# A graph-network layer on one core: a new order on ScalarE and VectorE in the edge pass, and a third of the edge dots on VectorE

## The chip, the cores and the metric

The kernel runs on one core of a Trainium2 chip. The metric is the device time of one execution in microseconds (us). TensorE (PE in the profile) multiplies matrices, VectorE (DVE) and ScalarE (ACT) work on rows, GpSimd (POOL) issues the gathers and scatters by index, and SyncE (SP) issues the plain transfers. Every engine works through its own instructions in order and waits on semaphores for the others.

## The reference

50,000 nodes with rows `x` of 256 values, 12,500 edges (`src`, `dst`, a feature row of 128 values each). Two layers, each followed by a normalisation of the rows:

```python
h = x @ Wn.T + bn
e = edge_attr @ We.T + be
a = leaky_relu(sum((h[src] + e) * attn, axis=-1), 0.01)
a = softmax of a over the edges with equal dst
x = layernorm(x + relu(segment_sum(h[src] * a, dst)))
agg = segment_sum(x[dst], src); mean = agg / max(count, 1)
x = layernorm(x + x @ W1.T + b1 + mean @ W2.T + b2)
```

The sum over `e * attn` is the dot of an edge's feature row with the single vector `We.T @ attn`, called u here. The 98 tiles of 128 edges (the last has 84) need one such dot per edge. In the second layer a node that occurs as `src` gets the mean over its neighbours; every other node gets only `x @ W1.T`.

## The kernel before, in words

Edges are handled in T = 100 tiles of 128 (two of them, or nearly so, are padding), four tiles to a group, Q = 25 groups. The program runs through these stages:

1. **Sorting by dst.** VectorE and ScalarE write one-hot tables (`onehots`, `high_onehots`), and TensorE counts them into a histogram (`sort`, `count_tile`). In the same loop TensorE makes the dots of the edge features: `turn_edges` transposes four tiles, ScalarE copies the result out of PSUM (`copy_edges`), `dot_edges` multiplies by u. SyncE loads the feature rows in chunks of eight tiles into the four `yout` buffers (`load_edges`) and puts parts of a copy of x between them (`copy_x`, 125 parts of 400 KB in all). VectorE waits in `edge_dots` for all dots, copies them to `pay`, and then scans the histogram (`starts`). The look-up of each edge's rank follows (`tiles`), and GpSimd scatters the ranked edges.
2. **Sorting by src**, the same without the edge features; GpSimd gathers the rows `x[src]` meanwhile, and VectorE dots them (`v_b`).
3. **DST pass**: softmax, weighted sums by dst, relu, added to the copy of x in DRAM.
4. **Dense pass**: all 98 groups of 512 node rows: normalise, multiply by W1, normalise, store.
5. **SRC pass** (`by_src` on four engines, 25 groups): the mean over neighbours for the nodes that occur as `src`, whose output rows are then overwritten by scatter.

In the SRC pass a step q of TensorE works on two groups. For each half p of a group (two tiles of 128) it transposes the own rows of group h = q - 1 (line 1378, "turn"), sums the neighbours of group q into `bank[2 + p]` (line 1533, "sums"), and multiplies both parts of group h by W2 and W1 (line 1389, "products"). The products of half p wait for ScalarE's copy of the turned rows (`own_copy(p)`, line 586, semaphore `s_tcc`). ScalarE also normalises the own rows (line 770), weighs the neighbour rows (line 750), takes square roots (`root`, line 591) and writes the output rows (`y_rows`, line 596). VectorE takes means and variances (line 971: of own rows, of neighbour rows, of the products), builds the selection matrices (`select_src`, lines 1058 to 1065), computes the scales of the own rows (lines 985 and 801) and adds the carry from tile to tile (`sums_with_carry`, line 801, which waits for the products that read its output before). GpSimd gathers the own rows of a group four steps ahead (line 484) and scatters the finished rows (line 487), eight transfers to a step.

The order on each engine is the order in which the code of `by_src` is written; there is no scheduler. In ScalarE's step the first instruction is the square root for the own rows of group q, which waits for VectorE:

```python
if in_range(q, 0, Q):
    root(u % 2, s_ost, q + 1, s_osq)
own_copy(0)
```

and in VectorE's loop the statistics behind that root come right after `sums_with_carry` of the step before.

## Time and profile before

| | us |
|---|---|
| median of 3 runs (1404.85 to 1406.67) | 1405.91 |
| the profiled execution's own time | 1415.9 |
| its span, first to last instruction | 1414.1 |
| TensorE busy in the span | 1201.5 (85%) |
| VectorE busy | 1002.8 (71%) |
| ScalarE busy | 745.4 (53%) |
| GpSimd busy | 751.7 (53%) |

The profile shows one execution on the chip. Times count from the span's start. The granted clock of TensorE is given as a share of full speed, 1.0 for 2.4 GHz and 0.5 for 1.2 GHz; a stretch that holds some of both shows a value between. The sort by dst takes the span's first 180 us or so, the DST pass runs from about 390 to 600 us, the dense pass from about 615 to 1053 us and the SRC pass from 1056 us to the end.

### The profile page before, as it was taken

What the parts mean: (1) busy time and instruction counts of PE and PEld (TensorE: products, weight loads), DVE (VectorE), ACT (ScalarE), POOL (GpSimd) and SP (SyncE); (2) the same over time, 40 slices, a digit from 0 to 9 for tenths busy, and PEclk for the clock granted to TensorE, in tenths of its full rate; (3) what the DMA queues carried; (4) which work ended last, traced back from release to release, by engine and by line L of the source; (5) the groups of instructions that cost most, each with busy time, mean ns of one, the idle gap of its engine ahead of it and who ended that gap; (6) DMA issues with size and microseconds to landing.
All of it is one profiled execution on the core that took longest, in us unless ns stands there. A gap on an engine that the chain in (4) does not pass through costs nothing.

```text
span 1414.1 us, 25043 instructions
## 1 busy us (share of the span) xinstructions
PE 1201.5 (85%) x6829; PEld 1046.3 (74%) x6829; DVE 1002.8 (71%) x3483; ACT 745.4 (53%) x1743; POOL 751.7 (53%) x731
## 2 busy tenths in 40 slices
PE   5988968991099999949999999999988888888884
PEld 5977857880078888838888888888877777777773
DVE  8377897989455555349999999999985556555551
ACT  3754664550034444427777766667674544545442
POOL 1047772777767777744444106555541555555533
PEclk9989999996589999979999999999998889988887
DMA  6868887979436666657777768999961323222211
GB/s 213 272 150 206 208 225 184 272 231 348 171 68 93 101 94 92 72 137 246 239 240 245 248 241 296 310 321 325 325 238 51 91 94 94 86 91 88 93 47 43
DMA packets 118160, 254.11 MB, mean 180 GB/s; under 512 B 23705, under 2 KB 63272, under 8 KB 118084
## 3 DMA queue, kind: packets, MB, share of 16 engines
q1 hardware_dynamic: 75738, 187.26, 41.8%
q0 software_dynamic: 40128, 64.45, 20.1%
q10 hardware_dynamic: 2218, 1.53, 0.3%
q8 instruction: 30, 0.49, 0.2%
q14 instruction: 46, 0.38, 0.1%
HBM read 175.67 MB, written 130.44 MB: 216 GB/s over the span
## 4 chain that ended last, share of the span: by engine, by line
PE 70%; DVE 11%; DMA 6%; ACT 5%; issue 5%; POOL 1%; SPq 0%; DVEq 0%; ACTq 0%; POOLq 0%
PE bank L1389 41%; PE bank L1378 8%; PE bank L1366 5%; DVE stats L971 4%; PE bank L1438 3%; PE bank L1288 3%; PE bank L1442 3%; DMA X<-in_x,idx_src 3%; DVE X L798 2%; ACT aggn L633 2%; PE bank L1533 2%; ACT sel L687 1%; PE bank L1325 1%; DVE xT L801 1%; DVE xin L798 1%
## 5 line engine op out<-in xcount | busy, mean ns | idle before, releaser
L1389 PE MATMUL bank<-w1T,xT 128*128 128x256 f32 x1968 | 480.3, 392 | 2.0 <-ACT yout L596 2.0
L1389 PEld LDWEIGHTS bank<-w1T,xT 128*128 128x128 f32 x1968 | 378.0, 197 | 56.6 <-ACT xT L586 3.0
L494 POOL DMA_INDIRECT order_scratch<-pay,rank_i x200 | 194.6, 973 | 220.6 <-DVE xin L798 90.3
L586 ACT ACTIVATE xT<-bank 128x512 f32<-128x512 f32 x296 | 176.7, 598 | 91.5 <-PE bank L1378 87.0
L596 ACT ACTIVATE yout<-bank,rstd 128x256 f32<-128x256 f32 x492 | 203.8, 480 | 0.7 <-DVE rstd L1037 0.5
L591 ACT ACTIVATE std<-stats,eps_c 128x4 f32<-128x4 f32 x271 | 80.5, 298 | 230.5 <-DVE stats L971 230.4
L534 POOL DMA_INDIRECT z_scratch<-xin,idx_out x100 | 156.3, 1563 | 53.8 <-ACT xin L713 30.6
L971 DVE BATCH_NORM_STATS2 stats<-bank 128x6 f32<-128x512 f32 x246 | 167.9, 691 | 10.2 <-PE bank L1389 10.1
L971 DVE BATCH_NORM_STATS2 stats<-xin 128x6 f32<-128x512 f32 x240 | 154.6, 686 | 22.6 <-DMA xin<-z_scratch 22.6
L1389 PE MATMUL bank<-w2T,xT 128*128 128x256 f32 x400 | 126.7, 446 | 50.4 <-ACT xT L586 41.8
L487 POOL DMA_INDIRECT out_rows<-yout,idx_out x100 | 102.4, 1024 | 107.7 <-ACT yout L596 83.0
L1366 PE MATMUL bank<-sel,agg 128*128 128x196 f32 x800 | 157.0, 341 | 0.1
L801 DVE SCALAR_TENSOR_TENSOR xT<-csel,xT,bank 128x128 f32<-128x128 f32 x198 | 55.6, 342 | 139.4 <-PE bank L1389 126.3
L1378 PE MATMUL bank<-ident,xin 128*128 128x128 f32 x960 | 128.9, 274 | 19.6 <-DVE xin L798 19.6
L1378 PEld LDWEIGHTS bank<-ident,xin 128*128 128x128 f32 x960 | 114.3, 142 | 34.4 <-issue 19.9
L1389 PEld LDWEIGHTS bank<-w2T,xT 128*128 128x128 f32 x400 | 84.9, 222 | 69.2 <-issue 31.8
L798 DVE TENSOR_SCALAR xin<-xin,stats,rstd 128x256 f32<-128x256 f32 x392 | 136.0, 409 | 0.1
L1366 PEld LDWEIGHTS bank<-sel,agg 128*128 128x128 f32 x800 | 134.4, 196 | 0.6 <-DVE bank L801 0.3
L484 POOL DMA_INDIRECT X<-z_scratch,idx_dst x100 | 96.1, 961 | 69.1 <-DVE xin L798 29.7
L484 POOL DMA_INDIRECT X<-in_x,idx_src x100 | 99.0, 990 | 51.2 <-issue 20.7
L484 POOL DMA_INDIRECT xin<-z_scratch,idx_src x88 | 84.7, 963 | 76.2 <-PE bank L1378 53.8
L1288 PE MATMUL bank<-X 128*128 128x196 bf16 x800 | 96.2, 255 | 28.8 <-ACT sel L687 18.6
(249 smaller groups left out, 1765.7 us busy)
## 6 DMA issues: line engine op xcount, KB each, us to landing
z_scratch<-in_x SPq DMA_DIRECT2D x125, 400.0 KB
xin<-z_scratch SPq DMA_DIRECT2D x97, 512.0 KB, 4.8
out_rows<-yout SPq DMA_DIRECT2D x97, 512.0 KB, 3.7
kB<-sorted_scratch SPq DMA_DIRECT2D x50, 256.0 KB, 3.4
yout<-low_digits_scratch SPq DMA_DIRECT2D x50, 128.0 KB
yout<-keys_scratch SPq DMA_DIRECT2D x50, 128.0 KB, 5.7
yout<-in_edge_attr SPq DMA_DIRECT2D x12, 512.0 KB, 6.2
order_scratch<-pay,rank_i POOLq DMA_INDIRECT x200
```

The costliest lines, as they stand in the source:

```text
L484: g.indirect_dma_start(out=dst_ap, out_offset=None, in_=table, in_offset=where).then_inc(s, 16)
L487: g.indirect_dma_start(out=table, out_offset=where, in_=src_ap, in_offset=None, bounds_check=N - 1, oob_is_err=False).then_inc(s, 16)
L494: g.indirect_dma_start(out=order_dram[k], out_offset=bass.IndirectOffsetOnAxis(ap=rank_i[k][:, t:t + 1], axis=0), in_=pay[:, t, :], in_off ...
L534: g.indirect_dma_start(out=z_dram, out_offset=column(idx_out[DST], GT * q + j), in_=xin[q % 4][:, j, :], in_offset=None, compute_op=ALU.ad ...
L586: a.activation(xT[dst_i][:].rearrange("p a b c -> p (a b c)"), src_bank[:, :], ACT.Copy, bias=raised).then_inc(copied, 1)
L596: a.activation(yout[hu][0:rows, j, :], bank_of(j // 2)[0:rows, (j % 2) * D:(j % 2 + 1) * D], ACT.Copy, scale=rstd[0:rows, slot, j:j + 1]). ...
L798: return v.tensor_scalar(o, i, s1, s2, o0, o1) if o1 is not None else v.tensor_scalar(o, i, s1, s2, o0)
L971: return v.bn_stats(stats[0:rows, slot, 2 * p:2 * p + 2, :].rearrange("p j s -> p (j s)"), pair.rearrange("p j c -> p c j"))
L1288: ins = mm(o[:, b * HC:(b + 1) * HC], onehot_lo[:, t, b * P:(b + 1) * P], onehot_hi[:, t, :], start=False, stop=False, skip_group_check=True)
L1366: ins = mm(bank[3 + t % 4][:, 0:HC], onehotT[n % 2][:, b, j * P:(j + 1) * P], table[i % 2][:, b, :], start=b == 0, stop=b == 1)
L1378: ins = tr(o[:, at:at + n], buf[0:n, 2 * p + jj, c * P:(c + 1) * P], ident[0:n, 0:n])
L1389: ins = mm(to, buf[:, jj, c, 0:n], w[:, c, :], start=not bias and i == 0 and c == 0, stop=i == len(terms) - 1 and c == 1)
```

## The change

It has two parts. In the SRC pass ScalarE and VectorE execute the same instructions in another order. ScalarE's step begins with the copy of the first turned half, and the square root for the own rows is made one group ahead (q + 1 in place of q); the output rows are written in two halves with the second copy between them. VectorE begins its step with the statistics of the products, then takes the own rows' statistics of group q + 1. The first group's own rows are done ahead of the loop.

```diff
+            root(0, s_ost, 1, s_osq)
             weigh_neighbours(0, 0)
...
-                if in_range(q, 0, Q):
-                    root(u % 2, s_ost, q + 1, s_osq)
                 own_copy(0)
-                if in_range(q, 2, Q + 2):
-                    root(2 + u % 2, s_est, q - 1, s_esq)
-                own_copy(1)
                 if in_range(q, 0, Q):
                     act.wait_ge(s_onm, q + 1)
...
+                if in_range(q, 2, Q + 2):
+                    root(2 + u % 2, s_est, q - 1, s_esq)
                 if in_range(q, 0, Q - 1):
-                    weigh_neighbours(q + 1, u + 1)
-                if in_range(q, 0, Q - 2):
-                    root_neighbours(q + 2, u)
+                    root((u + 1) % 2, s_ost, q + 2, s_osq)
                 if in_range(q, 2, Q + 2):
...
-                    y_rows(0, hu, 2 + u % 2, s_ey, lambda p: rbank(u % 2, p))
+                last_step(0)
+                own_copy(1)
+                last_step(1)
+                if in_range(q, 0, Q - 1):
+                    weigh_neighbours(q + 1, u + 1)
+                if in_range(q, 0, Q - 2):
+                    root_neighbours(q + 2, u)
```

One step of ScalarE's queue in the SRC pass, as it was (the step of group 3: `xT2` and `xT3` are the copies of the two turned halves, `std` is a square root, `xin1` the own rows, `X` the weighed neighbours, `yout1` the output rows):

```order
L591 ACTIVATE std<-stats,eps_c 128x4
L586 ACTIVATE xT2<-bank0 128x512
L591 ACTIVATE std<-stats,eps_c 128x4
L586 ACTIVATE xT3<-bank1 128x512
L770 ACTIVATE xin1<-xin1,nmr,rstd 128x256 x4
L750 ACTIVATE X<-X,rstd 128x256 x4
L591 ACTIVATE std<-stats,eps_c 128x4
L596 ACTIVATE yout1<-bank6,rstd 128x256 x2
L596 ACTIVATE yout1<-bank7,rstd 128x256 x2
```

The same step of ScalarE in the changed kernel (lines 600, 785, 605, 610 and 765 are the former 586, 770, 591, 596 and 750):

```order
L600 ACTIVATE xT2<-bank0 128x512
L785 ACTIVATE xin1<-xin1,nmr,rstd 128x256 x4
L605 ACTIVATE std<-stats,eps_c 128x4 x2
L610 ACTIVATE yout1<-bank6,rstd 128x256 x2
L600 ACTIVATE xT3<-bank1 128x512
L610 ACTIVATE yout1<-bank7,rstd 128x256 x2
L765 ACTIVATE X<-X,rstd 128x256 x4
L605 ACTIVATE std<-stats,eps_c 128x4
```

The first copy no longer has a square root ahead of it in its step; the second copy has moved behind the normalising, two square roots and half of the output rows.

VectorE's step of group 2 as it was, up to the first addition of the carry (`aggn` holds own rows, `bank4` and `bank5` products, `X` neighbour rows):

```order
L971 BN_STATS stats<-aggn 128x6 x2
L1058 RECIPROCAL rstd<-std 128x4
L1060 TENSOR_TENSOR rstd<-rstd,weight 128x4
L1063 TENSOR_TENSOR csel1<-kB1,prevk1 128x512
L1065 TENSOR_TENSOR sel1<-kB1,keyc1 128x512
L985 RECIPROCAL rstd<-std 128x4
L801 SCALAR_TENSOR_TENSOR nmr<-stats,rstd 128x4
L971 BN_STATS stats<-bank4 128x6
L971 BN_STATS stats<-bank5 128x6
L971 BN_STATS stats<-X 128x6 x2
L1250 RECIPROCAL rstd<-std 128x4
L801 SCALAR_TENSOR_TENSOR xT0<-csel0,xT1,bank2 128x128 x2
```

and in the changed kernel:

```order
L998 BN_STATS stats<-bank4 128x6
L998 BN_STATS stats<-bank5 128x6
L998 BN_STATS stats<-xin1 128x6 x2
L1281 RECIPROCAL rstd<-std 128x4
L1085 RECIPROCAL rstd<-std 128x4
L1087 TENSOR_TENSOR rstd<-rstd,weight 128x4
L1090 TENSOR_TENSOR csel1<-kB1,prevk1 128x512
L1092 TENSOR_TENSOR sel1<-kB1,keyc1 128x512
L1012 RECIPROCAL rstd<-std 128x4
L822 SCALAR_TENSOR_TENSOR nmr<-stats,rstd 128x4
L998 BN_STATS stats<-X 128x6 x2
L822 SCALAR_TENSOR_TENSOR xT0<-csel0,xT1,bank2 128x128 x2
```

The statistics of the products lead the step, and those of the own rows are of group 3 (`xin1`) in place of group 2 (`aggn`).

The second part concerns the edge dots in the sort by dst. TensorE keeps the tiles 0 to 63 and the last two (66 tiles, 17 groups in place of 25). The other 32 tiles are loaded by SyncE in four transfers into the `xin` buffers, and VectorE multiplies each with u, spread over all partitions (`u_b`, made by two more products of TensorE and a copy by ScalarE), and sums along the row. Three parts of x are copied after a chunk in place of two.

```diff
+            for i in range(4):
+                load_rest(i)
-            for c in range(4, NEC + FT + 1 - NEC * EC):
+            for c in range(4, len(EDGE_CHUNKS)):
                 sp.wait_ge(s_eaT, 2 * (c - 3))
                 load_edges(c)
-                copy_x(2)
+                copy_x(3)
...
+            a.copy(u_b[:], bank[3][:, D:D + DE])
...
-                dve.wait_ge(s_ead, Q)
-                v.tensor_copy(pay[:, 0:FT, 2], bank[0][:, 0:FT])
+                dve.wait_ge(s_wcp, 4)
+                dve.wait_ge(s_er4, 64)
+                for t in range(NPE * EC, NEC * EC):
+                    f = edge_rest[t // EC - NPE][:, t % EC, :]
+                    stt(f, f, 1.0, u_b[:], ALU.mult, ALU.mult, accum_out=pay[:, t:t + 1, 2])
+                dve.wait_ge(s_ead, len(EDGE_GROUPS))
...
             for b in range(2):
+                mm(bank[3][:, D:D + DE], attn_b[:, b, :], weT[:, b, :], start=b == 0, stop=b == 1)
```

The end of TensorE's counting loop in the changed kernel, from the last full group of edge tiles on (1353 turns edge tiles, 1326 counts, 1360 makes dots, 1322 closes the histogram):

```order
L1353 MATMUL bank4<-ident,yout3 128x128 x4
L1326 MATMUL bank7<-X 128x196 x8
L1360 MATMUL bank0<-u_c,xT2 128x1 x4
L1353 MATMUL bank3<-ident,yout0 128x128
L1353 MATMUL bank3<-ident,yout1 128x84
L1326 MATMUL bank7<-X 128x196 x8
L1360 MATMUL bank0<-u_c,xT3 128x1 x4
L1326 MATMUL bank7<-X 128x196 x8
L1360 MATMUL bank0<-u_c,xT2 128x1
L1360 MATMUL bank0<-u_c,xT2 84x1
L1326 MATMUL bank7<-X 128x196 x56
L1322 MATMUL bank7<-zero16 128x392
```

Before, every group of counts up to the last had its turns and dots beside it; now the last 56 counting products, seven groups, stand alone.

## Rows read from the trace of the kernel before

**Rows 1.** Stretches: busy of PE, PEld, DVE, ACT, POOL; PEclk, DMA share, GB/s
```profile
25.00:50.00 25.00, 25.00 (x254) 24.87 (x253) 23.30 (x115) 17.73 (x39) 0.00 (x0) 1.00 0.94 317
1200.00:1225.00 25.00, 20.67 (x106) 17.77 (x105) 13.04 (x37) 13.43 (x33) 13.91 (x15) 0.90 0.29 85
```
**Rows 2.** Timeline of PE, SRC pass: start us, us, instruction [idle before <-releaser]
```profile
1063.29 1.10 PE L1389 MATMUL bank<-w2T,xT 128*128 128x256 f32 x4 [1.07 <-issue]
...
1202.01 0.60 PE L1378 MATMUL bank<-ident,xin 128*128 128x128 f32 x4
...
1206.85 0.60 PE L1378 MATMUL bank<-ident,xin 128*128 128x128 f32 x4
...
1210.60 1.13 PE L1389 MATMUL bank<-w2T,xT 128*128 128x256 f32 x4 [2.26 <-ACT xT L586]
...
1215.84 0.60 PE L1378 MATMUL bank<-ident,xin 128*128 128x128 f32 x4
...
1220.84 0.60 PE L1378 MATMUL bank<-ident,xin 128*128 128x128 f32 x4
...
1386.34 1.10 PE L1389 MATMUL bank<-w2T,xT 128*128 128x256 f32 x4 [0.73 <-DVE xT L801]
```
**Rows 3.** Timeline of ACT, one step of the SRC pass
```profile
1209.67 0.30 ACT L591 ACTIVATE std<-stats,eps_c 128x4 f32<-128x4 f32 x1 [1.25 <-DVE stats L971]
1209.87 0.59 ACT L586 ACTIVATE xT<-bank 128x512 f32<-128x512 f32 x1
...
1216.56 0.60 ACT L586 ACTIVATE xT<-bank 128x512 f32<-128x512 f32 x1 [3.21 <-PE bank L1378]
1217.05 2.06 ACT L770 ACTIVATE xin<-xin,nmr,rstd 128x256 f32<-128x256 f32 x4
1219.02 1.69 ACT L750 ACTIVATE X<-X,rstd 128x256 f32 x4
...
1220.80 1.53 ACT L596 ACTIVATE yout<-bank,rstd 128x256 f32<-128x256 f32 x4
```
**Rows 4.** Timeline of DVE, one step of the SRC pass
```profile
1207.21 1.12 DVE L801 SCALAR_TENSOR_TENSOR xT<-csel,xT,bank 128x128 f32<-128x128 f32 x4 [3.71 <-PE bank L1389]
1208.34 1.30 DVE L971 BATCH_NORM_STATS2 stats<-xin 128x6 f32<-128x512 f32 x2
...
1211.72 1.30 DVE L971 BATCH_NORM_STATS2 stats<-bank 128x6 f32<-128x512 f32 x2
```
**Rows 5.** Short stretches, columns as in rows 1
```profile
189.70:216.20 26.50, 16.95 (x161) 12.40 (x161) 26.44 (x140) 13.25 (x32) 20.40 (x21) 1.00 1.01 272
...
1210.60:1214.70 4.10, 4.10 (x13) 3.35 (x14) 3.65 (x9) 0.30 (x1) 3.12 (x3) 0.65 0.55 139
```
**Rows 6.** Groups by line in the SRC pass: busy us, mean ns | idle before
```profile
L487 POOL DMA_INDIRECT out_rows<-yout,idx_out x100 | 102.4, 1024 | 107.7 <-ACT yout L596 83.0 <-issue 24.8
...
L484 POOL DMA_INDIRECT xin<-z_scratch,idx_src x81 | 77.7, 959 | 60.2 <-PE bank L1378 39.6 <-issue 20.6
```
**Rows 7.** Timeline of POOL: a gather while the DMA engines are full
```profile
340.28 1.08 POOL L484 DMA_INDIRECT X<-in_x,idx_src x1 [0.31 <-DMA X<-in_x,idx_src]
```
**Rows 8.** Timeline of PE in the sort by dst: two groups of edge tiles
```profile
65.44 0.63 PE L1318 MATMUL bank<-ident,yout 128*128 128x128 f32 x4
...
67.42 0.63 PE L1318 MATMUL bank<-ident,yout 128*128 128x128 f32 x4
```
**Rows 9.** Timeline of ACT in the sort by src: one-hots without edge copies between
```profile
181.76 0.44 ACT L633 ACTIVATE aggn<-iota,dig_f 128x196 bf16<-128x196 bf16 x1
...
182.60 0.44 ACT L633 ACTIVATE aggn<-iota,dig_f 128x196 bf16<-128x196 bf16 x1
```
**Rows 10.** Timeline of DVE in the sort by dst
```profile
71.79 0.29 DVE L840 COPY pay<-bank 128x97 f32<-128x97 f32 x1 [23.32 <-PE bank L1325]
...
75.39 0.35 DVE L801 SCALAR_TENSOR_TENSOR xT<-yout,pay,earlier_mask 128x128 f32<-128x128 uint16 x1
75.66 0.08 DVE L801 DVE_READ_ACCUMULATOR xT<-yout,pay,earlier_mask 128x1 f32 x1
```

More of the change, by code:

```diff
@@ L73, in build @@
     NEC = FT // EC
+    NPE = NEC - 4
+    EDGE_CHUNKS = [(c * EC, EC) for c in range(NPE)] + [(t, 1) for t in range(NEC * EC, FT + 1)]
+    EDGE_GROUPS = [[t + i for i in range(k)][h:h + GT] for t, k in EDGE_CHUNKS[:NPE] for h in range(0, k, GT)] \
+        + [[t for t, k in EDGE_CHUNKS[NPE:]]]
+    assert len(EDGE_GROUPS[-1]) <= GT
     NCOPY, CR = 125, 5
@@ L108, in build @@
         u_c = sb("u_c", [P, 1])
+        u_b = sb("u_b", [P, DE])
         c0 = sb("c0", [P, 1])
@@ L186, in build @@
         edge_rows = [t[:].rearrange("p j c -> p (j c)").rearrange("p (t d) -> p t d", d=DE) for t in yout]
+        edge_rest = [t[:].rearrange("p j c -> p (j c)").rearrange("p (t d) -> p t d", d=DE) for t in xin]
         edge_turned = [xT[2 + i][:].rearrange("p a b c -> p (a b c)") for i in range(2)]
@@ L359, in load_edges @@
             def load_edges(c):
-                if c < NEC:
+                t, k = EDGE_CHUNKS[c]
+                if k == EC:
                     v = edge_attr[0:NEC * EC * P].rearrange("(c t p) d -> p c t d", p=P, t=EC)
@@ L675, in _ @@
                     high_onehots(k, q)
-                    if k == DST:
+                    if k == DST and q < len(EDGE_GROUPS):
                         copy_edges(q)
@@ L1229, in _, with own_stats, own_offsets @@
             n_m = [G // 2 + (i % 2 < G % 2) for i in range(4)]
+            def own_stats(q, m, u):
+                own = own_rows(q, u)
+                dve.wait_ge(s_xs[u % 4], 16 * GT * (m + u // 4 + 1))
+                moments(u % 2, lambda p: own[:, 2 * p:2 * p + 2, 0:D], P, s_ost)
+            def own_offsets(q, m, u):
+                slot = u % 2
+                dve.wait_ge(s_osq, q + 1)
+                invert(slot, P, n_m[slot] + counted(m, u, 0, 2) + 1)
+                stt(nmr[:, slot, :], stats[:, slot, :, 1], -1.0, rstd[:, slot, :], ALU.mult, ALU.mult).then_inc(s_onm, 1)
+            own_stats(0, 0, 0)
+            own_offsets(0, 0, 0)
             def by_src(q, m, u):
                 slot = u % 2
-                if in_range(q, 0, Q):
-                    own = own_rows(q, u)
-                    dve.wait_ge(s_xs[u], 16 * GT * (m + 1))
-                    moments(slot, lambda p: own[:, 2 * p:2 * p + 2, 0:D], P, s_ost)
-                if in_range(q, 0, Q - 1):
-                    select_src(q + 1, m, u, 1)
-                if in_range(q, 0, Q):
-                    dve.wait_ge(s_osq, q + 1)
-                    invert(slot, P, n_m[slot] + counted(m, u, 0, 2) + 1)
-                    stt(nmr[:, slot, :], stats[:, slot, :, 1], -1.0, rstd[:, slot, :], ALU.mult, ALU.mult).then_inc(s_onm, 1)
                 if in_range(q, 2, Q + 2):
@@ L1245, in by_src @@
                     moments(2 + slot, lambda p: halves(rbank(slot, p)[:, :]), P, s_est)
[L1246 to L1247 removed]
+                if in_range(q, 0, Q - 1):
+                    own_stats(q + 1, m, u + 1)
                 if in_range(q, 2, Q + 2):
@@ L1250, in by_src @@
                     v.reciprocal(rstd[:, 2 + slot, :], std[:, 2 + slot, :]).then_inc(s_enm, 1)
+                if in_range(q, 0, Q - 1):
+                    select_src(q + 1, m, u, 1)
+                    own_offsets(q + 1, m, u + 1)
+                if in_range(q, 0, Q - 2):
+                    neighbour_stats(q + 2, u)
                 if in_range(q, 0, Q):
@@ L1276, in _ @@
                 mm(bank[3][:, 0:D], attn_b[:, b, :], xin[0][:, b, :], start=b == 0, stop=b == 1)
+            for b in range(2):
+                mm(bank[3][:, D:D + DE], attn_b[:, b, :], weT[:, b, :], start=b == 0, stop=b == 1)
             for b in range(2):
@@ L1303, in shift_ordered @@
                 mm(o[:, 3 * P:3 * P + T], lastrow[:], keyc[k][:, 0:T], start=True, stop=True).then_inc(s_next, 1)
-            def edge_tiles(g):
-                return range(GT * g, min(GT * g + GT, FT + 1))
             def edge_rows_of(t):
@@ L1311, in turn_edges @@
             def turn_edges(g):
-                for t in edge_tiles(g):
-                    c, i = (t // EC, t % EC) if t < NEC * EC else (NEC + t - NEC * EC, 0)
+                for j, t in enumerate(EDGE_GROUPS[g]):
+                    c, i = (t // EC, t % EC) if t < NPE * EC else (NPE + t - NEC * EC, 0)
                     pe.wait_ge(s_ea[c % 4], 16 * (c // 4 + 1))
-                    n, j = edge_rows_of(t), t % GT
+                    n = edge_rows_of(t)
                     if j == 0:
@@ L1322, in dot_edges @@
                 pe.wait_ge(s_eac, g + 1)
-                for t in edge_tiles(g):
-                    n, j = edge_rows_of(t), t % GT
+                for j, t in enumerate(EDGE_GROUPS[g]):
+                    n = edge_rows_of(t)
                     ins = mm(bank[0][0:n, t:t + 1], edge_turned[g % 2][:, j * P:j * P + n], u_c[:], start=True, stop=True)
@@ L1333, in sort @@
                     if t % GT == 0:
-                        if k == DST:
+                        if k == DST and t // GT < len(EDGE_GROUPS):
                             turn_edges(t // GT)
@@ L1338, in sort @@
                     count_tile(hist, t)
-                    if k == DST and t % GT == GT - 1 and t > GT:
+                    if k == DST and t % GT == GT - 1 and 1 <= t // GT <= len(EDGE_GROUPS):
                         dot_edges(t // GT - 1)
-                if k == DST:
-                    dot_edges(Q - 1)
                 nothing(hist, start=False, stop=True).then_inc(s_hist, 1)
```

14 lines of the change are left out of this document (10 added, 4 removed).

## The prediction

> **What bounds the kernel now.** I read the stretches first, then the chain that ended last, then the timelines of TensorE, ScalarE and VectorE in one step of the SRC pass. In the SRC pass no engine is full: TensorE is busy 20.67 of 25 us, at a granted clock of 0.90, and every other engine less [rows 1]. From the first products to the last group's it takes 1386.34 - 1063.29 = 323.05 us for 24 steps, 13.46 us each [rows 2]. The timeline of TensorE shows where they go. A half step (turn, sums, products) that runs through lasts 4.84 us (from 1202.01) or 5.00 us (from 1215.84). The other half, from 1206.85 to 1215.84, lasts 8.99 us [rows 2]. Its products waited 2.26 us for ScalarE's copy `xT`. Then they ran slowly: the 4.1 us after the wait have a granted clock of 0.65, so most of them went by at 1.2 GHz [rows 5]. Of the 3.99 us that this half is longer, 2.26 are the wait and 1.73 the clock.
>
> Why is that copy late? ScalarE's rows say it: the copy at 1209.87 had its input early, but stood behind the square root at 1209.67, which waited for VectorE's statistics [rows 3]. Those started at 1208.34, right after the addition of the carry at 1207.21, which itself can only start when the last products of the step before are done [rows 4]. So once a step TensorE's end goes through VectorE (carry, own statistics) and ScalarE (root, copy) before its next products may start. The second copy, at 1216.56, has nothing ahead of it, and its half shows no such wait.
>
> In the sort by dst the bound is TensorE again: a group with edge tiles takes 67.42 - 65.44 = 1.98 us [rows 8], TensorE is full and its clock is 1.00 [rows 1]. VectorE meanwhile waits 23.32 us for the dots, until 71.79 [rows 10].
>
> **The change in the SRC pass.** The instructions stay; three queues must be laid out anew. I count from the start of a step's first turn, and take a step of two halves that run through, 2 x 4.92 = 9.84 us.
>
> ScalarE: the first copy starts 0.72 us after its turn (1215.84 to 1216.56) [rows 2, 3], then the own rows follow at 1.21 and take 1.97 (1217.05 to 1219.02), to 3.2; the root for the products at 3.2; the root for the next own rows when VectorE has them, at 4.0 (below), to 4.3; half of the 1.53 us of output rows to 5.1; the second copy at 4.92 + 0.72 = 5.64, when its turn is done; the other output rows to 6.9; the neighbour rows, 1.69, to 8.6; the last root to 8.9. The next step's first copy is due at 9.84 + 0.72 = 10.56. ScalarE has 1.6 us to spare, and 0.5 us before the second copy [rows 3].
>
> VectorE: the second half's carry starts 0.36 us after the turn (1207.21 against 1206.85) and takes 1.13, to 1.5; the statistics of the products 1.30, to 2.8; own statistics, selection and scales as before 1211.72 - 1208.34 = 3.38, of which the statistics end at 4.0 and the rest at 6.2; a reciprocal and the neighbour statistics, as long as the products', to 7.7; the first half's carry to 8.8 [rows 2, 4]. It then waits for the last products, at 9.84 + 0.36. There are 1.4 us to spare. That carry is what the next step's sums wait for, and they are due at 9.84 + 0.5.
>
> What is queued behind the moved waits: VectorE now begins by waiting for the last products of the step before, but the carry before it waits for the same products, so nothing is held longer. The own statistics are a group ahead, so they wait for a gather one step earlier. Ahead of the loop, the first own rows' root and scales add a wait of VectorE of up to 2 us for ScalarE's last output rows of the dense pass; the first sums wait for the neighbour rows there anyway, and I take 0 (at most 2).
>
> GpSimd becomes the closest. A scatter and a gather are 1.02 and 0.96 us, and some 0.3 us lie between two that wait for little [rows 6, 7], so eight cost 4 x 1.32 + 4 x 1.26 = 10.3 us a step, 0.5 more than TensorE. It does not bind: the first scatter follows the first output rows, 6.9 us into step 2, and the gather behind it ends 10.3 us later, while VectorE reads those rows 2.8 us into step 5, 3 x 9.84 - 6.9 + 2.8 = 25.4 us after. That is 15 us of lead less the landing, and 18 further gathers lose 18 x 0.5 = 9 of it.
>
> So 24 x (13.46 - 9.84) = **87 us** off. Bounds: with halves of 5.00 us 83, with 4.84 us 91; if GpSimd's 10.3 us ruled every step, 76.
>
> **The change in the sort.** 17 groups have edge tiles instead of 25. The eight others need only TensorE's counts and ScalarE's one-hots; those take 182.60 - 181.76 = 0.84 us a group where nothing is between them [rows 9]. That is 8 x (1.98 - 0.84) = 9.1 us less. VectorE's 32 dots have no row of their own: a product with a running sum on 128 x 128 starts its read-out 0.27 us after it starts, and takes 0.43 with both in full [rows 10], so 9 to 14 us. VectorE has been idle since 71.79 - 23.32 = 48.5, so the dots end at 57 to 62, and the histogram closes near 72 - 8 = 64: hidden, but if that cover were gone the whole 9 to 14 would show. `u_b` costs two products ahead of the loop, each like a turn's (0.63 for four, twice that at the lower clock) and a copy of at most 0.6 [rows 3, 8]: 0.3 to 1.3 us, on the path; I take 1.
>
> SyncE's queue is the risk. Four loads of 512 KB go in front, and a chunk is followed by three parts of 400 KB instead of two. The last tile is due at 65.44 - 6 x 1.98 + 1 = 54.6. Before it, from about 22 us on, pass 8 chunks of 512 KB and 15 parts, 10.3 MB, at the 317 GB/s of that stretch [rows 1] 32.5 us: it lands at 54.5. So this costs 0 to 4 us; I take 0. The sort gains **8 us**, between 3 and 9. The later stages start earlier by that much; two parts of x less have been copied by then, and the last 31 instead of 29 run beside GpSimd's gathers, as now, at 1.38 us instead of 1.26 each [rows 5, 7], so two more parts cost less than 1 us.
>
> The sum: 87 + 8 = 95 us. The profiled execution took 1415.9 us, 10 above the median of the runs; it would become 1321, and the median 1405.9 - 95 = **1311 us**.
>
> **The rivals.**
> *GpSimd sets the pace.* VectorE will work 8.8 of 9.8 us instead of 13 of 25, beside GpSimd's transfers. A gather took 1.08 us, 1.38 with the gap, in another stretch [rows 7]; with that for all, a step is 11.0 us, 1.2 behind TensorE, and after 12 steps the lead is gone. The transfers alone then end 6 us later; if TensorE waits 1.2 us in each of the last ten steps and its clock falls (1.73), 30 us: 1317 to 1341. For it: GpSimd has the least to spare. Against it: in a stretch with VectorE busy 26.44 of 26.5 us GpSimd still issued 21 transfers, one in 1.26 us [rows 5]. 15%. The Trainium skill (SBUF — State Buffer, "Who interferes with whom") has a rule that makes this case: a VectorE instruction with two inputs in SBUF, as the two selections of a step are, holds a port that a reading GpSimd instruction needs, and the later of the two waits until the other ends; that would slow the transfers as VectorE fills up. The stretch just named, with its one-input instructions, does not test the rule, and no other row here does.
>
> *The wait comes back at the second copy.* It now stands behind output rows that wait for VectorE's reciprocal, 0.5 us before it is due. If VectorE is 1.6 us late there, 1.1 us a step return, 24 x 1.1 = 26 us: 1337. With a wait and clock loss as now, 24 x 3.6 = 87, only the sort's gain is left: 1398. For it: a longer chain (own statistics, reciprocal, rows) in front of the copy. Against it: each piece is short and its inputs are early by the layout. 10%.
>
> *Both halves wait, and the clock falls in both.* Then a step loses 2 x (w + 1.73) instead of 3.62; it is slower than before from w = 0.25 us on (the sort's 8 us are 0.33 a step), and with w = 2.26 as now it costs 24 x 4.4 = 105 more than before: 1503. Against it: 161 counting products, 20 groups of eight, ran a stretch of 26.5 us at clock 1.00 though TensorE was busy only 16.95 us, so 0.48 us were idle in each group [rows 5], so short waits alone do not bring the clock down; and two long waits do not follow from the layout. 3%.
>
> *The order changes nothing that ends last*, and the sort's gain is lost in later waits for transfers: 1406, 2%.
>
> **How the numbers follow.** The forecast (1300 to 1317, its own bounds) has 70%, GpSimd's pace 15%, the second copy 10%, both halves 3%, nothing 2%. The range takes in the first two, 1299 to 1341. About 0.2% is what a measurement of this kernel can tell from no change: faster by more than that 95%, within it 2%, slower by more than it 3%.
>
> **What would show it.** Right: in the SRC pass steps of 9.7 to 10.0 us, a granted clock near 1.0, no wait of the products for `xT` over 0.3 us, GpSimd nearly back to back; the histogram's scan near 64 us, the dots on VectorE done before. Wrong: a wait of 1 us or more before either half's products, own statistics that wait for a gather, steps over 10.5 us, or a count in the sort that waits for an edge chunk.

## The result and the profile after

The changed kernel takes **1320.2 us** (median, 1315.6 to 1322.2) against 1405.4 us of the kernel before in the same comparison, a ratio of **0.939 (95% interval 0.9363 to 0.9416)**, 85 us less. The forecast was 1311, the range 1299 to 1341. Its profiled execution took 1320.2 us (span 1318.4); the one before took 1415.9, so the two traces differ by 95.7 us, which is the 95 of the sum, while the medians differ by 85. Some executions take about 45 us longer than the others of the same kernel, whichever kernel it is (two of the seven of e1, two of the six of e3), and the medians and ratios of this document leave them out.

The parts of the page for the changed kernel, engine shares:

```profile
PE 1150.3 (87%) x6737; PEld 1008.8 (77%) x6737; DVE 1008.6 (77%) x3548; ACT 740.3 (56%) x1736; POOL 754.0 (57%) x731
```

Stretches of the changed kernel, columns as in [rows 1]:

```profile
50.00:75.00 25.00, 20.93 (x149) 18.62 (x148) 10.43 (x71) 13.49 (x29) 0.00 (x0) 0.74 0.45 132
...
1200.00:1225.00 25.00, 25.00 (x145) 22.28 (x144) 20.38 (x56) 17.75 (x44) 19.21 (x20) 1.00 0.37 114
...
1270.00:1280.00 10.00, 9.21 (x53) 8.09 (x52) 5.78 (x18) 6.17 (x16) 7.56 (x9) 1.00 0.26 86
```

In the middle of the SRC pass TensorE is now busy all 25 us at a granted clock of 1.00, where [rows 1] had 20.67 at 0.90. GpSimd issues 20 transfers in that stretch. The last line is from the end of the pass, where TensorE waits a little again; the first is the sort by dst, with a clock of 0.74.

TensorE's timeline in one step of the SRC pass, to set beside [rows 2]:

```profile
1199.46 0.60 PE L1411 MATMUL bank<-ident,xin 128*128 128x128 f32 x4
1199.90 1.06 PE L1566 MATMUL bank<-sel,X 128*128 128x128 f32 x8
1200.94 1.13 PE L1422 MATMUL bank<-w2T,xT 128*128 128x256 f32 x4
...
1204.49 0.60 PE L1411 MATMUL bank<-ident,xin 128*128 128x128 f32 x4
```

No wait stands ahead of the products, and the half from 1199.46 to 1204.49 lasts 5.03 us. The first products of the pass and those of the last group:

```profile
1053.32 1.89 PE L1422 MATMUL bank<-w2T,xT 128*128 128x256 f32 x4
...
1290.71 1.10 PE L1422 MATMUL bank<-w2T,xT 128*128 128x256 f32 x4 [0.73 <-DVE xT L822]
```

Between them go 237.39 us, 9.89 for each of 24 steps, against 323.05 and 13.46 before; 21 of the steps lie between 9.69 and 9.91 us.

ScalarE in the same step, to set beside [rows 3] (L600 is the copy, L605 the root, L785 the own rows, L610 the output rows):

```profile
1200.20 0.60 ACT L600 ACTIVATE xT<-bank 128x512 f32<-128x512 f32 x1 [1.84 <-PE bank L1411]
1200.69 2.06 ACT L785 ACTIVATE xin<-xin,nmr,rstd 128x256 f32<-128x256 f32 x4
1202.66 0.28 ACT L605 ACTIVATE std<-stats,eps_c 128x4 f32<-128x4 f32 x1
1203.49 0.30 ACT L605 ACTIVATE std<-stats,eps_c 128x4 f32<-128x4 f32 x1 [0.55 <-DVE stats L998]
...
1205.21 0.60 ACT L600 ACTIVATE xT<-bank 128x512 f32<-128x512 f32 x1 [0.69 <-PE bank L1411]
```

In this step both copies wait for TensorE's turn, and for nothing else. VectorE in the same step, beside [rows 4]:

```profile
1199.82 1.12 DVE L822 SCALAR_TENSOR_TENSOR xT<-csel,xT,bank 128x128 f32<-128x128 f32 x4 [1.73 <-PE bank L1422]
1200.95 1.30 DVE L998 BATCH_NORM_STATS2 stats<-bank 128x6 f32<-128x512 f32 x2
1202.17 1.29 DVE L998 BATCH_NORM_STATS2 stats<-xin 128x6 f32<-128x512 f32 x2
```

It still waits for the last products (1.73 us), but what follows, the statistics, is no longer in front of the first copy.

In the sort by dst, TensorE's timeline of the changed kernel, where the last edge tiles are turned (beside [rows 8]):

```profile
53.68 0.30 PE L1353 MATMUL bank<-ident,yout 128*128 128x128 f32 x1
55.34 0.40 PE L1353 MATMUL bank<-ident,yout 84*128 84x84 f32 x1 [1.35 <-DMA yout<-in_edge_attr]
55.53 1.51 PE L1326 MATMUL bank<-X 128*128 128x196 bf16 x8
56.84 1.76 PE L1360 MATMUL bank<-u_c,xT 128*128 128x1 f32 x8
...
60.34 5.56 PE L1326 MATMUL bank<-X 128*128 128x196 bf16 x56
```

The last tile is late: TensorE waits 1.35 us for it, and the eight counts and eight dots behind it take 1.51 and 1.76 us, nearly twice the 0.84 and 0.97 of the group ahead (at 52.17 and 52.84 in this trace). The ranks begin (the product with `csel` and the identity, L1383) at 68.81 us, 6.3 before the 75.13 of the kernel before. VectorE's dots, beside [rows 10]:

```profile
48.20 0.29 DVE L822 SCALAR_TENSOR_TENSOR xin<-xin,u_b 128x128 f32<-128x128 f32 x1
48.42 0.08 DVE L822 DVE_READ_ACCUMULATOR xin<-xin,u_b 128x1 f32 x1
...
60.51 0.24 DVE L866 COPY pay<-bank 128x64 f32<-128x64 f32 x1 [5.42 <-PE bank L1360]
```

The 32 go from 48.20 to 55.0, and VectorE then waits 5.42 us for TensorE's.

At the end of the pass GpSimd's lead is used up. VectorE, ScalarE and TensorE of the changed kernel in the last steps:

```profile
1262.51 1.30 DVE L998 BATCH_NORM_STATS2 stats<-xin 128x6 f32<-128x512 f32 x2 [1.49 <-DMA xin<-z_scratch,idx_src]
```

```profile
1263.84 0.30 ACT L605 ACTIVATE std<-stats,eps_c 128x4 f32<-128x4 f32 x1 [2.03 <-DVE stats L998]
...
1264.76 0.59 ACT L600 ACTIVATE xT<-bank 128x512 f32<-128x512 f32 x1
```

```profile
1265.41 1.13 PE L1422 MATMUL bank<-w2T,xT 128*128 128x256 f32 x4 [0.64 <-ACT xT L600]
...
1276.10 1.13 PE L1422 MATMUL bank<-w2T,xT 128*128 128x256 f32 x4 [0.79 <-ACT xT L600]
```

Three times VectorE waits for gathered rows (3.9 us in all). The root of the own rows is late by that, and with it the second copy, which stands behind it: after the turn at 1263.28 it was due at 1264.0, and it starts at 1264.76. Twice TensorE waits for it, and two steps last 10.53 and 10.70 us. The clock stays at 1.00 through these short waits.

### The profile page after: what moved, and what is told of

Its sections match the earlier page's. It is cut to its first block, busy times and chain, and to the rows that moved or that the text cites. A ratio compares the mean times of both kernels' runs of the same rounds, so it can differ in the third digit from the quotient of the medians.

```text
span 1318.4 us, 24909 instructions
## 1 busy us (share of the span) xinstructions
PE 1150.3 (87%) x6737; PEld 1008.8 (77%) x6737; DVE 1008.6 (77%) x3548; ACT 740.3 (56%) x1736; POOL 754.0 (57%) x731
## 4 chain that ended last, share of the span: by engine, by line
PE 69%; DVE 9%; DMA 8%; issue 5%; ACT 4%; POOL 3%; SPq 0%; ACTq 0%; POOLq 0%; DVEq 0%
PE bank L1422 39%; PE bank L1411 9%; PE bank L1399 5%; PE bank L1471 3%; PE bank L1475 3%; DMA X<-in_x,idx_src 3%; PE bank L1566 3%; PE bank L1326 3%; DVE stats L998 3%; DMA yout<-low_digits_scratch 3%; DVE X L819 3%; ACT aggn L648 2%; ACT sel L702 1%; DVE xin L819 1%; POOL out_rows L501 1%
## 5 line engine op out<-in xcount | busy, mean ns | idle before, releaser
L1422 PE MATMUL bank<-w1T,xT 128*128 128x256 f32 x1968 | 460.9, 380 | 1.8 <-ACT yout L610 1.8
L1422 PEld LDWEIGHTS bank<-w1T,xT 128*128 128x128 f32 x1968 | 365.5, 190 | 50.4 <-ACT xT L600 2.2
L600 ACT ACTIVATE xT<-bank 128x512 f32<-128x512 f32 x296 | 177.2, 599 | 73.0 <-PE bank L1411 68.7
L610 ACT ACTIVATE yout<-bank,rstd 128x256 f32<-128x256 f32 x492 | 206.7, 481 | 1.4 <-DVE rstd L1281 0.7
L605 ACT ACTIVATE std<-stats,eps_c 128x4 f32<-128x4 f32 x271 | 80.4, 298 | 163.6 <-DVE stats L998 163.5
L822 DVE SCALAR_TENSOR_TENSOR bank<-iota_f,dig_f,bank 128x196 f32<-128x196 f32 x200 | 84.5, 423 | 33.5 <-PE bank L1399 33.4
L1422 PE MATMUL bank<-w2T,xT 128*128 128x256 f32 x400 | 107.5, 391 | 2.9 <-ACT xT L600 1.4
L1326 PEld LDWEIGHTS bank<-X 128*128 128x128 bf16 x800 | 67.8, 100 | 55.1 <-ACT sel L702 33.2
```

The costliest lines, as they stand in the source:

```text
L600: a.activation(xT[dst_i][:].rearrange("p a b c -> p (a b c)"), src_bank[:, :], ACT.Copy, bias=raised).then_inc(copied, 1)
L610: a.activation(yout[hu][0:rows, j, :], bank_of(j // 2)[0:rows, (j % 2) * D:(j % 2 + 1) * D], ACT.Copy, scale=rstd[0:rows, slot, j:j + 1]). ...
L1326: ins = mm(o[:, b * HC:(b + 1) * HC], onehot_lo[:, t, b * P:(b + 1) * P], onehot_hi[:, t, :], start=False, stop=False, skip_group_check=True)
L1422: ins = mm(to, buf[:, jj, c, 0:n], w[:, c, :], start=not bias and i == 0 and c == 0, stop=i == len(terms) - 1 and c == 1)
```

## The experiments

There are eleven runs; e7 and e9 are the kernel before and the changed kernel once more. Each ratio is to the kernel before, in runs on the same chip. The theory was that of the prediction: ScalarE's first copy stood behind a root that hung on TensorE's own last products. What had to be told apart was whether the copy's place alone did it, what each part gave, and what GpSimd costs now.

| run | median us | ratio (95% interval) |
|---|---|---|
| changed kernel | 1320.2 | 0.939 (0.9363 to 0.9416) |
| e1_order | 1324.7 | 0.942 (0.9406 to 0.9435) |
| e2_edges | 1403.2 | 0.9972 (0.996 to 0.9985) |
| e3_copy_first | 1339.4 | 0.9516 (0.9502 to 0.9531) |
| e4_root_ahead | 1407.0 | 0.9989 (0.9969 to 1.0009) |
| e5_last_tile | 1314.2 | 0.9336 (0.9314 to 0.9359) |
| e6_half_scatter | 1311.2 | 0.932 (0.9293 to 0.9346) |
| e8_one_input | 1316.8 | 0.9359 (0.9335 to 0.9383) |
| e9_after_again | 1316.7 | 0.9345 (0.9327 to 0.9362) |
| e10_both | 1314.0 | 0.9329 (0.9309 to 0.9348) |
| e11_forty | 1308.9 | 0.9295 (0.9278 to 0.9311) |

### Each part alone

**e1_order** is the kernel before with the diff's parts in ScalarE's and VectorE's `by_src` (and the own root and statistics ahead of the loop); **e2_edges** is the kernel before with all other parts of the diff.

> The kernel before with the new order of the SRC pass alone; the sort by dst stays as it was. The trace of the changed kernel has 24 steps of 9.88 us there, 86 us less than the profiled execution before; by the medians both parts together take off 85. If the parts add, the sort has some 6 to 10 of that, and this kernel takes 1326 to 1330 us, with steps of 9.7 to 9.9 us. Rival, that the sort's gain is lost later and all of the 85 is the order's: 1320.

> The kernel before with the edge dots divided between VectorE and TensorE alone; the SRC pass keeps its old order. The changed kernel's trace is 6.3 us ahead when the sort's ranks begin, and 9.8 us ahead at the first products of the SRC pass. If that is the edge part's alone, 1396 to 1399 us. Rival, that the gain is taken back by waits for transfers further on: 1403 to 1406.

Measured: e1 takes off 0.058 of 1405.9, 81.5 us (79 to 84), e2 0.0028, 3.9 us (2 to 6). Together 85.4, and the whole change 85.8 (0.061): the parts add. So the order of the SRC pass is 95% of the gain; 81.5 off is 1324.4, just under the 1326 to 1330 expected of e1, and the rival's 1320 is outside the interval. The edge part is worth about half of what was expected of e2; its ranks begin at 66.44 us, and it too waits for the last tile, 1.26 us. Against e3 and e7, whose sort is the old one, its ranks are 6.4 us ahead (72.84 and 72.88 there), but the first products of its SRC pass only 3.7 and 4.9 us (1054.20 against 1057.85 and 1059.12). So a part of the gain is lost on the way, as the rival had it; where, no run here settles.

### One line, both ways

**e3_copy_first** moves one line in the kernel before:

```
 def by_src(q, m, u):
...
+    own_copy(0)
     if in_range(q, 0, Q):
         root(u % 2, s_ost, q + 1, s_osq)
-    own_copy(0)
     if in_range(q, 2, Q + 2):
         root(2 + u % 2, s_est, q - 1, s_esq)
```

> The kernel before with one line moved: ScalarE's first copy stands ahead of the square root of the own rows; nothing else of the new order. Theory A, the place of that copy is the whole cause: steps of 9.7 to 10.0 us, 1326 to 1331 us. Theory B, VectorE's order is needed too: the root of the products now comes only after own statistics, selection, scales and the products' statistics (1.5 + 1.3 + 1.5 + 0.4 + 1.3 = 6.0 us into the step), the second copy stands behind it (due at 5.6) and 5.8 us of rows behind that, so that the next first copy is late by nearly 2 us: steps of 11.6 us at full clock, 1361 us, and up to 13.3 with the clock's loss, 1402.

Measured: 0.0484 of 1405.9, 68 us, with steps of 10.49 us on average: the figure of neither theory, but much nearer to theory A. ScalarE's timeline of this kernel (L586 copy, L591 root, L770 own rows, L750 neighbour rows, L596 output rows):

```profile
1198.50 0.30 ACT L591 ACTIVATE std<-stats,eps_c 128x4 f32<-128x4 f32 x1 [2.92 <-DVE stats L971]
1198.79 0.60 ACT L586 ACTIVATE xT<-bank 128x512 f32<-128x512 f32 x1
1199.28 2.06 ACT L770 ACTIVATE xin<-xin,nmr,rstd 128x256 f32<-128x256 f32 x4
1201.25 1.69 ACT L750 ACTIVATE X<-X,rstd 128x256 f32 x4
...
1203.04 1.53 ACT L596 ACTIVATE yout<-bank,rstd 128x256 f32<-128x256 f32 x4
1204.46 0.59 ACT L586 ACTIVATE xT<-bank 128x512 f32<-128x512 f32 x1
```

and what TensorE makes of it:

```profile
1205.10 1.13 PE L1389 MATMUL bank<-w2T,xT 128*128 128x256 f32 x4 [0.61 <-ACT xT L586]
```

The root of the products comes 5.9 us after the turn at 1192.56, where theory B had it at 6.0, and behind it ScalarE works without a gap for 6.0 us, to the first copy of the next step, which makes TensorE wait 0.61 us. Theory B counted that delay as 2 us. With the wait cut from 2.1 to 0.6 us the clock stayed at 1.00, so the step is 10.5 instead of 13.6 us. The other 13.5 us (81.5 less 68) are what the rest of the new order gives; in the changed kernel's rows the root of the products stands at 3.2 us after the turn, ahead of the second copy, and output rows fill the time in which ScalarE here waits 2.92 us.

**e4_root_ahead** moves one line in the changed kernel, and lets the first copy hang on VectorE again:

```
+    if in_range(q, 2, Q + 2):
+        root(2 + u % 2, s_est, q - 1, s_esq)
     own_copy(0)
     if in_range(q, 0, Q):
         act.wait_ge(s_onm, q + 1)
...
-    if in_range(q, 2, Q + 2):
-        root(2 + u % 2, s_est, q - 1, s_esq)
```

> The changed kernel with one line moved back: ScalarE's square root of the products' statistics stands ahead of the first copy again, so that this copy waits for carry and statistics on VectorE after the last products (1.5 + 1.3 us after the turn, where the copy is due at 0.7). Theory A, a copy behind a root is the whole cause: the first products wait some 2.4 us a step and the clock falls (1.7): 24 steps of 13.8 us, 1418 us; with the wait alone, and the clock at 1.0, 24 x 2.4 = 58 more, 1378. Rival, that VectorE's order makes the gain and the copy's place does not matter: 1320, no wait for the copy over 0.3 us.

Measured: 1407 us, a ratio of 0.9989 (0.9969 to 1.0009). Of 85.8 us one line has taken back 84. ScalarE's and TensorE's timelines of this kernel:

```profile
1203.41 0.30 ACT L605 ACTIVATE std<-stats,eps_c 128x4 f32<-128x4 f32 x1 [3.93 <-DVE stats L998]
1203.62 0.58 ACT L600 ACTIVATE xT<-bank 128x512 f32<-128x512 f32 x1
```

```profile
1204.34 1.78 PE L1422 MATMUL bank<-w2T,xT 128*128 128x256 f32 x4 [2.25 <-ACT xT L600]
```

The wait is 2.0 to 2.3 us in each step, as [rows 2] had it, and the products behind it run slowly again (1.78 for four that take 1.13). Seven of the 24 steps last 11.9 to 12.6 us, the other 17 13.5 to 13.9, 13.23 on average. That the expected 1418 was not reached is those seven: the clock did not fall in each step.

### The kernel before once more

> The kernel before once more, for a second trace. Its first profiled execution took 1415.9 us at a mean clock of 0.925, its other executions some 10 us less at 0.927 to 0.935. If those 10 us were the clock's, this trace has a higher clock and steps of the SRC pass under 13.4 us; if they lay in the transfers of the first stages, its steps are 13.4 to 13.5 us and the scan of the sort by dst ends earlier.

It took 1406.7 us at a mean clock of 0.930. Its 24 steps took 318.1 us instead of 323.05, with the same waits (41.8 us in 20 waits for the copy, as in the first trace). Stretches of this run and two products in them:

```profile
1090.00:1115.00 25.00, 20.87 (x97) 17.78 (x96) 14.35 (x38) 12.48 (x32) 15.07 (x15) 0.86 0.35 101
...
1165.00:1190.00 25.00, 20.57 (x115) 18.25 (x116) 16.35 (x44) 13.89 (x35) 16.37 (x18) 1.00 0.31 94
```

```profile
1177.33 1.13 PE L1389 MATMUL bank<-w2T,xT 128*128 128x256 f32 x4 [2.06 <-ACT xT L586]
```

From 1165 to 1190 the clock is 1.00 although TensorE waits 2.06 us a step as elsewhere, and the four products take 1.13 us, the full speed. Such steps last 11.4 to 12.2 us, those with the fall 13.5 to 13.8. In the first trace three steps were short, here six. Of the 9.2 us between the two profiled executions 5.0 lie in these steps; 2.3 are there when the ranks of the sort by dst begin (75.13 against 72.88), and 3.5 at the first scatter into `z_scratch` (407.6 against 404.1). So both explanations that the expectation set against each other hold in part.

### What GpSimd costs now

**e6_half_scatter** leaves out two of the four scatters of output rows in each group but the last, so that half of these rows are not written (the counts that wait for them are halved with it):

```
-for j in range(GT):
+for j in range(GT if h == Q - 1 else 2):
     scatter(out, yout[h % 4][:, j, :], column(idx_out[SRC], GT * h + j), s_ysc[h % 4])
```

> The changed kernel with two of the four scatters of output rows left out in every group but the last, so that half the output is not written: GpSimd has 6 transfers a step, 7.7 us, instead of 8. Theory: in the changed kernel GpSimd needs 10.5 us a step where TensorE needs 9.7, its lead runs out only three steps before the end, and costs the waits of 0.64 and 0.79 us seen there: own statistics wait for no gather, TensorE is full to the last step, 1318 to 1319 us. Rival A, that GpSimd holds TensorE back over the whole pass: over 10 us less. Rival B, that the three waits are hidden: no difference, 1320.

VectorE's waits for gathers and TensorE's waits for the copy are gone, and the 24 steps take 235.39 us instead of 237.39; 1.9 us of that in steps 21 to 23 (31.08 to 29.18). So GpSimd's pace costs the changed kernel 2 us at the end of the pass, and nothing ahead of it. That the median is lower by more has two other reasons. The spans of the two traces differ by 9.0 us (1318.4 and 1309.4). 2.8 of them lie ahead of the first products, in stages which this edit does not touch (the ranks of its sort begin at 65.82, those of the changed kernel at 68.81). And 4.2 lie at the very end: from the first products of the last group to the end of the span go 27.73 us in the changed kernel and 23.49 here. They are the last instruction of GpSimd's queue, a DRAIN (duration in ns, start in us), in the changed kernel

```profile
L88 POOLq DRAIN  x1: 8237/8237/8237, 1310.0 to 1310.0; - x1
```

and in this run:

```profile
L88 POOLq DRAIN  x1: 3991/3991/3991, 1305.2 to 1305.2; - x1
```

It takes 8.24 us in every other trace, that of the kernel before included, each with 702 transfers by index; here there are 654. On what its length hangs is not shown. So the 9 us do not speak for rival A.

**e8_one_input** replaces the two comparisons of a selection:

```
-v.tensor_tensor(csel[par][:], kB[par][:], prevk[SRC][:, now].unsqueeze(2).to_broadcast([P, GT, P]), ALU.is_equal)
-v.tensor_tensor(sel[par][:], kB[par][:], keyc[SRC][:, now].unsqueeze(2).to_broadcast([P, GT, P]), ALU.is_equal).then_inc(s_sel[SRC], 1)
+for o, col in ((csel, prevk), (sel, keyc)):
+    for j in range(GT):
+        ins = ts(o[par][:, j, :], kB[par][:, j, :], col[SRC][:, bass.ds(q * GT + j, 1)], None, ALU.is_equal)
+ins.then_inc(s_sel[SRC], 1)
```

> The changed kernel with VectorE's two selections of a step (128x512, two inputs in SBUF, 0.61 us apart) each written as four comparisons with one column (128x128, one input and a scalar, 0.26 us apart as in the pass by dst): 2.1 us instead of 1.2 for the same result. In the changed kernel all 21 of GpSimd's transfers that begin within a selection take 1.22 us on average, the 133 others 0.98. Theory, the two-input instruction holds up the transfer's start: now none is over 1.1 us, GpSimd's eight take 10.3 us instead of 10.5, the lead lasts longer, and the time is within 2 us of 1320. Rival, that these transfers are long for another reason, as their place in a group: the same lengths as before. VectorE has 1.7 us to spare a step, so its 0.9 more should not show; if it does, steps of over 10 us.

GpSimd's groups by line in the SRC pass from 1075 to 1272 us (busy us, mean ns | idle before), first the changed kernel:

```profile
L501 POOL DMA_INDIRECT out_rows<-yout,idx_out x75 | 77.6, 1034 | 22.8 <-issue 22.2 <-ACT yout L610 0.6
L498 POOL DMA_INDIRECT xin<-z_scratch,idx_src x76 | 74.9, 985 | 23.2 <-issue 21.9 <-PE bank L1411 0.6 <-ACT yout L610 0.6
```

and this run:

```profile
L501 POOL DMA_INDIRECT out_rows<-yout,idx_out x77 | 77.5, 1006 | 23.5 <-issue 22.5 <-ACT yout L610 0.9
L498 POOL DMA_INDIRECT xin<-z_scratch,idx_src x76 | 73.1, 961 | 23.6 <-issue 22.2 <-PE bank L1411 0.8 <-ACT yout L610 0.6
```

A transfer has become 26 ns shorter on average ((77.6 + 74.9) / 151 against (77.5 + 73.1) / 153), 0.2 us for the eight of a step. The 24 that begin within a selection now take 1.01 us on average (at most 1.13), where 21 took 1.22; the theory holds, but not to the last tenth. The own statistics wait for no gather any more, the last four steps take 9.69 to 9.80 us, the 24 steps 235.54. VectorE's longer selections (1.6 us instead of 1.2, less than the 2.1 expected) do not show. The time itself, 1316.8, can't be told from the changed kernel's (ratios 0.9359, 0.939 and, in e9, 0.9345, with intervals that overlap).

### A version that beats both

**e5_last_tile** is one line in SyncE's queue:

```
 for c in range(4, len(EDGE_CHUNKS)):
     sp.wait_ge(s_eaT, 2 * (c - 3))
     load_edges(c)
-    copy_x(3)
+    copy_x((3, 3, 2, 1, 0, 9)[c - 4])
```

> The changed kernel with fewer parts of x ahead of the last two edge tiles in SyncE's queue (9 instead of 15; the other nine follow behind them, the number stays). In the changed kernel's trace TensorE waits 1.35 us for the last tile, and then 8 counts and 8 dots run at half the clock, 2.1 us more, while ScalarE's one-hots are ahead. Theory: the wait is the parts' place in the queue: the last turn waits under 0.3 us, the sort's seed comes 2 to 3 us earlier, 1317 to 1318 us. Rival, that ScalarE's one-hots (0.84 us a group) end the stage anyway: within 1 us of 1320.

TensorE's timeline in the sort by dst:

```profile
52.61 0.38 PE L1353 MATMUL bank<-ident,yout 128*128 128x128 f32 x2
52.88 0.83 PE L1326 MATMUL bank<-X 128*128 128x196 bf16 x8
...
64.23 0.93 PE L1383 MATMUL bank<-csel,ident 128*128 128x392 f32 x2 [1.04 <-DVE csel L822]
```

Both tiles are there at once, the clock does not fall, and the ranks begin at 64.23. In six traces with the old place of the loads (the changed kernel, e2, e4, e6, e8 and e9) the last turn waits 0.9 to 1.5 us, and the ranks begin at 65.7 to 70.1, 67.4 on average. So the lateness cost some 3 us. How much of it the time shows can't be read from medians on different chips; hence the next three ran side by side.

> The changed kernel once more, on the chip and beside the runs that it is to be compared with. From its first runs 1316 to 1322 us; the last turn in the sort waits 1.0 to 1.5 us for its edge tile, as in the four traces with these loads.

> The changed kernel with both edits: fewer parts of x ahead of the last edge tiles, and the selections as one-input comparisons. If the two add (3.6 us from the sort's seed at 64.2 instead of 67.8 on average, 2.1 us from the SRC pass, 697.1 instead of 699.2 from the last scatter into z to the last products), 5 to 6 us less than the changed kernel on this chip. Rival, that VectorE's 0.8 us more a step brings a wait back in some step: 3.6 or less.

**e10_both** is e5 and e8 together. **e11_forty** also has `NPE = NEC - 5`, and two more row buffers (half of `aggn`, and `kB[1]`) for the eight tiles:

```
-NPE = NEC - 4
+NPE = NEC - 5
...
+edge_more = [aggn[:, 0:2, :].rearrange("p j c -> p (j c)").rearrange("p (t d) -> p t d", d=DE), kB[1][:]]
...
-    copy_x((3, 3, 2, 1, 0, 9)[c - 4])
+    copy_x((3, 2, 1, 0, 12)[c - 4])
```

> The kernel of e10_both with 40 instead of 32 edge tiles on VectorE, the eight more in two other row buffers. Theory: TensorE has two groups less with edge tiles, 2 x (1.98 - 0.84) = 2.3 us; VectorE's dots go from 48.5 to 57.0 us at 0.213 us each, before the counts close at 59, so 2 to 3 us less than e10_both. Rival A, that ScalarE's one-hots or the digits end the stage: no difference. Rival B, that the 512 KB more ahead of TensorE's later chunks make its turns wait: 1 us or more lost there, slower than e10_both.

The changed kernel took 1316.7 this time, a ratio of 0.9345 (0.9327 to 0.9362), a little less than at first; e10 1314.0, 2.7 us less and not the 5 to 6 expected. Its interval overlaps with that of the changed kernel, so the gain is shown by the traces alone: 24 steps in 234.64 us against 236.35, and ranks at 64.47 against 65.68. That is 1.2 us in the sort and not the 3.6 expected, since e9's last tile was the least late of all (0.91 us). No wait has come back in a step, so the rival's cause is not there. e11 took 1308.9, a ratio of 0.9295 (0.9278 to 0.9311), clear of the changed kernel: **7.8 us less**. TensorE and VectorE of e11 in the sort:

```profile
51.10 7.40 PE L1333 MATMUL bank<-X 128*128 128x196 bf16 x72
...
61.41 1.19 PE L1390 MATMUL bank<-csel,ident 128*128 128x392 f32 x2 [1.03 <-DVE csel L828]
```

```profile
56.46 0.23 DVE L873 COPY pay<-bank 128x56 f32<-128x56 f32 x1
```

VectorE's 40 dots end at 56.5, before the counts (58.5), and the ranks begin 3.1 us before those of e10, for 2.3 expected. Nothing waits for a chunk, so both rivals fall. The median is 5.1 us below that of e10, where 2 to 3 were expected; the rest is not explained.

## Why the prediction was right, and where it was off

**The number.** 1320.2 us lies inside the range, but above the forecast's own bounds (1300 to 1317), in the part that was there for GpSimd's pace (1317 to 1341). But GpSimd's pace cost 2 us (e6); the distance to 1311 comes from two terms of the sum, below (87 was 81.5, and 8 was 3.9). So the range held in part by luck.

**The cause.** Right, and shown from both sides: the copy behind the root (e3 takes 68 of 81.5 us with that line alone, e4 gives back 84 with one line). The layout stands as it was counted from the turn (1199.46 in the rows above): first copy at 0.72, measured 0.74; next own root at 4.0, measured 4.03; second copy at 5.64, measured 5.75; VectorE's spare time 1.4, measured 1.73. The step was put at 9.84 and is 9.69 to 9.91 in 21 of the 24.

**The rivals.** The rival of both halves did not come. GpSimd's pace came in small: 18 gathers were to use 9 of 15 us of lead less the landing, and the lead did end, some three steps before the end, since a step took GpSimd 10.53 us (18 steps from 1076.99 to 1266.52) and not 10.3. It cost 2 us (e6), not the 6 to 30 of that rival, since TensorE's waits came in two steps and not in ten, and the clock did not fall. The ten did not fit the rival's own figures either: with the lead gone after 12 of 18 gathers, six steps were left. The rival of the second copy came only behind GpSimd's: in three steps (copies at 1254.16, 1264.76 and 1275.45) that copy stood behind the own root and output rows, and TensorE waited for it in two; elsewhere it waits for nothing but its turn. So four of the signs of being wrong, or near it, were seen, all small: own statistics that wait for a gather, three steps over 10.5 us (10.51 for the first of the pass, and the two of 10.53 and 10.70), waits for `xT` over 0.3 us, and a last edge tile that comes late in the sort.

**The sum against its own trace.** 87 for the SRC pass; the two traces give 323.05 - 237.39 = 85.7. 8 for the sort; the traces give 10.0 at the first products (1063.29 against 1053.32). 95 in all, 95.7 measured, and 1321 for the profiled execution, 1320.2 measured. This agreement is partly luck, as the next two points show.

**First term that was off: "the median 1405.9 - 95".** The sum was taken from the median as it stood, though the profiled execution was 10 us above it. Part of those 10 us was the very loss that the change removes: the clock fell in 21 of 24 steps there, in 18 of 24 in e7, and the 3.99 us of wait (2.26) and clock (1.73), read from one step, stood for all. In time the order gives 81.5 us (e1), not 87; with e7's steps in place of the first trace's the traces say the same, 318.07 - 237.39 = 80.7. The wait is 2.1 to 2.3 us in each step; the 1.7 of the clock come only where it fell. That the profiled execution took 10 us more than the median was the hint that it might hold more of this loss than most (its mean clock of 0.925, against 0.930 in e7, agrees), and the loss should have been scaled down.

**Second term that was off: "this costs 0 to 4 us; I take 0".** The last edge tile was put at 54.5 where it was due at 54.6, and it came at 55.3, due at 54.0. With a margin of 0.1 us out of 10 MB the mean of the bounds was the fairer choice: the sort gives 4 us by medians (e2) and some 5.5 in the traces (ranks at 67.4 on average against 72.8 to 72.9 in e3 and e7, whose sort is the old one), not 8. e5 shows the wait and the clock behind it gone when the tile is loaded earlier; its ranks, at 64.23, are then 8.6 us ahead of those of e3 and e7, so the other terms of that sum held when taken together.

**A term that was too dear, at no price.** VectorE's dots were put at 0.27 to 0.43 us each; they start every 0.213, since the read-out of one runs beside the start of the next. They were hidden either way, but this is why eight more fit (e11).

## What to carry to other kernels

When a busy engine waits once per step, follow the wait to the instruction that stands ahead of the late one in its queue: here one line with a root of 0.3 us cost 84 us when it was put back (e4), and gave 68 when a copy was moved ahead of it in the old order (e3); the rest of the new order was worth 13.5. If the profiled execution is slower than the median, find out where, before a sum from its trace is taken off the median; a loss that comes only in some steps is to be priced by how many. And a transfer whose landing is estimated within a tenth of a microsecond of its due time should not be priced at nothing: here it was late in all six traces.

## What the runs showed that was not expected

**The clock after equal waits.** A wait of 2.06 us was followed by products at half speed in most steps (granted clock 0.86 in the stretch at 1090) and by full speed for whole stretches (1.00 at 1165) in the same execution. After waits of 0.5 to 0.8 us it did not fall: it was 1.00 from 1060 to 1310 in e3, which has 22 of them there, and in the last steps of the changed kernel. In the sort it fell after a wait of 1.35 us, and in each of the five other traces with a late last tile, the shortest of whose waits was 0.91 us (e9).

**A transfer that begins within a selection.** Two of GpSimd's scatters in the changed kernel, and VectorE's second selection beside the later one:

```profile
1253.00 0.98 POOL L501 DMA_INDIRECT out_rows<-yout,idx_out  x1 [0.30 <-issue]
1254.29 1.32 POOL L501 DMA_INDIRECT out_rows<-yout,idx_out  x1 [0.30 <-issue]
```

```profile
1254.07 0.68 DVE L1092 TENSOR_TENSOR sel<-kB,keyc 128x512 f32<-128x512 f32 x1
```

The later one begins 0.46 us before the selection ends and is 0.34 us longer. From 1075 to 1276 all 21 transfers that began within a selection took 0.97 to 1.48 us, the longer the more of the selection was still to come (the longest met the end of the first selection and then the whole second one), and none of the 133 others took more than 1.1. The trace of the kernel before has it too: from 1075 to 1370 the 20 transfers that began within a selection took 1.15 us on average, the 140 others 0.98. The rule of the Trainium skill (SBUF — State Buffer, "Who interferes with whom"), that a VectorE instruction with two SBUF inputs holds up a reading GpSimd instruction which comes after it, agrees with this, and with e8, where one-input comparisons brought those transfers to 1.01 us. e8's instructions are also shorter (0.32 us instead of 0.69), but the length is not the cause: in the changed kernel 31 transfers began with more than 0.3 us still to come of a statistics instruction on `xin` or `X`, one input in SBUF and 0.69 us long, and took 0.98 us on average, at most 1.02. The price here is 0.2 us a step, where the rival in the prediction had GpSimd's step 0.7 us longer (11.0 instead of 10.3).
